# Attention and gated feed-forward block: transposed inputs, the keys' low part by DMA, and the products for the row maxima on 64 rows each

## The chip, the cores and the metric

One core of one Trainium2 chip runs the whole program. The metric is the device time of one execution in microseconds (us); less is better. The profile is of one execution. PE is TensorE, PEld its weight loads, DVE VectorE, ACT ScalarE, POOL GpSimd, SP the engine that issues most DMAs.

## The reference, cut to what matters

Eight batches, 100 query rows of 128, 1444 context rows of 64, 16 heads of 64.

```python
xh = layernorm(x)                                   # x: (8, 100, 128)
q, k, v = xh @ Wq, ctx @ Wk, ctx @ Wv               # ctx: (8, 1444, 64); 16 heads of 64
attn = softmax(q k^T / 8)                           # 100 x 1444 per head and batch
x = x + tanh(g_xattn) * ((attn v) @ Wo + bo)
y = layernorm(x)
h = silu(fp4(y) @ fp4(w_gate)^T) * (fp4(y) @ fp4(w_up)^T)
out = x + tanh(g_ffn) * fp4(h) @ fp4(w_down)^T      # fp4: blocks of 16, scale, round to a grid
```

## The kernel before, in words

**Folding.** The weights Wq and Wk are folded per head into one 128x64 matrix (`a_all`, key "A"), so the keys of every head are the context itself, and Wv with Wo into `vo`. The scores of a head are then (x_hat A_h) times the context.

**Precision.** Scores are exact to about float32 with reduced operands (float32r): the keys are split into a high part and a low part, so are the queries. `k_hl` holds on partitions 0 to 63 the high part and on 64 to 127 the low part of the transposed context (the rounding copies at L589, the low part at L911 on DVE); `k_h1` holds the high part and, below it, rows of ones (L588). `q_hh` holds the queries' high part twice, `q_ls` their low part and the shift.

**Groups and slots.** Work goes in 16 groups, half a batch's heads each (8 heads x 100 queries = 800 columns). A group has 24 slots: 12 chunks of 120 or 121 keys times two halves of 400 columns. A slot is two score products on PE (L793, 128 partitions, and L794, 71 partitions), then Exp on ACT into `probs` (L648). Two PSUM banks hold scores, so PE is at most two slots ahead of ACT. The product with the context (`attn_pair`, L807) writes one chunk to output partitions 0 to 63 and the other to 64 to 127; each of its float32 products is two records in the trace. Sums over keys are adds on DVE (L935) and POOL (L513).

**Maxima.** Exp needs a shift per query. While group g runs, PE makes for group g+1 the products for the maxima: 7 tiles of 116 queries times 3 parts of 482 keys = 21 products (L746, all 128 partitions: high and low part of the keys against the doubled queries). DVE reduces each (L915), then once more (L946), and a transpose (L749) and L917 put the shift into `q_ls`.

**Order of work.** Every engine has its own written program, walked slot by slot. What is not a score or an `attn_pair` is a use of one of four PSUM banks, a ring (`ring_keys`, `START`, `FINISH`, `ring_use` on each engine): the same list on each engine, and a bank is written again when the use four before it has been read (`ring_free`). The dictionaries `MAX_SLOTS`, `FFN_SLOTS`, `POST_SLOTS`, `CTX_SLOTS` and so on say by hand at which slot what is issued; on PE a slot is scores, ring uses, `attn_pair`. In the 24 slots of an even group the context of the next batch is transposed, in three uses of four transposes (L732).

**Start and end.** `START` transposes Wk, Wq, Wv on PE (L693, L685), makes A (L698) and `vo` (L704, operands on 64 partitions, of 0 to 63 and 64 to 127 in turn), the first keys, and the 21 maxima of group 0. `FINISH` is the feed-forward part of the last batch, a chain of small steps over DVE, POOL, ACT and PE.

Of the kernel before, what the change touches and what calls it, by code (L numbers as in the profile page):

```python
# [45 lines left out]
MAXC = [0, 482, 964, M]  # L46
PROBS = 6
# [3 lines left out]
SUM_P = [1, 2, 4, 5, 6, 7, 8]  # L51
# [14 lines left out]
MAX_SLOTS = {1: 1, 2: 1, 4: 1, 5: 2, 7: 3, 8: 2, 10: 2, 11: 2, 12: 1, 13: 2, 14: 1, 15: 1, 16: 1, 17: 1}  # L66
FFN_SLOTS = {2: ('zT', 0), 4: ('gate', 0), 6: ('up', 0)}
DOWN_SLOTS = {2: ('hT', 0), 3: ('hT', 1), 5: ('down', 0)}
LAST_FFN_SLOTS = {**FFN_SLOTS, 19: ('hT', 0), 20: ('hT', 1), 22: ('down', 0)}
W_SLOTS = {slot: ("wT", i) for i, slot in enumerate(LAST_FFN_SLOTS)}  # L70
POST_SLOTS = {6: ('sum', 0), 8: ('proj', 0), 10: ('proj', 1)}
CTX_SLOTS = {14: ('ctx', 0), 15: ('ctx', 1), 18: ('ctx', 2)}
XT_SLOT = 20
MAX_TILES_SLOT = 17
SHIFT_SLOT = 20


LN2_SLOTS = [12, 13]
LN2_APPLY_SLOT = 17
Z_SLOTS = [19, 19, 20, 21, 21, 21, 22, 22, 22]  # L80
SIGMOID_SLOTS = [5, 6]
H_SLOTS = [18, 19, 19, 20, 21, 21, 22, 22, 23]
LAST_H_SLOTS = [7, 8, 9, 10, 11, 12, 13, 14, 16]
ADD_LAG, LAST_ADD_SLOT = 3, 0


def ring_keys(g, slot):
    keys = []
    pre = g + 1 < GROUPS
    if pre and slot == 0:  # L90
# [19 lines left out]
START = [("wkT", 0), ("wqT", 0), ("xT", 0), ("A", 0), ("ctx", 0), ("q", 0), ("ctx", 1)]  # L110
BETWEEN = {1: ('ctx', 2), 4: ('wqT', 1), 7: ('A', 1), 9: ('wvT', 0), 13: ('vo', 0), 14: ('vo', 1), 16: ('vo', 2), 20: ('vo', 3)}
for _u in range(3 * TILES):
    START += ([BETWEEN[_u]] if _u in BETWEEN else []) + [("max", _u)]
START += [("shift", 0)]
FINISH = [("proj", 0), ("proj", 1), ("sum", 0), ("zT", 0), ("gate", 0), ("up", 0), ("hT", 0), ("hT", 1), ("down", 0)]
# [55 lines left out]
def xattn_ffn(nc, x, ctx_in, g_xattn, g_ffn, Wq, Wk, Wv, Wo, bo, w_gate, w_up, w_down, out):  # L171
    with ExitStack() as es:
# [18 lines left out]
        shift_mask = sb("shift_mask", [128, TILES, TROWS])  # L191
        tanh_x = sb("tanh_x", [128, 1])
# [21 lines left out]
        ctx_n = sb("ctx_n", [128, 2, CHUNKS, 2, C])  # L214
# [38 lines left out]
        wk_in = sem("wk_in")  # L253
        wq_in = sem("wq_in")
# [4 lines left out]
        ctx_loaded = [sem(f"ctx_loaded{i}") for i in range(2)]  # L259

# [9 lines left out]
        ctx_copied = sem("ctx_copied")  # L270
# [116 lines left out]
        def _(sp):  # L387
            def load_ctx(b, par):
                for i in range(2):
                    sp.dma_start(ctx_n[0:PFULL, par, :, i, :], ctx_in[b, 0:PFULL * CHUNKS, :].rearrange("(p c) d -> p c d", c=CHUNKS)).then_inc(ctx_loaded[par], 16)  # L390
                    sp.dma_start(ctx_n[PFULL:PFULL + 1, par, 0:EXTRA, i, :], ctx_in[b, PFULL * CHUNKS:M, :].rearrange("(p c) d -> p c d", c=EXTRA)).then_inc(ctx_loaded[par], 16)
# [27 lines left out]
            def group(t):  # L419
                if t.g % 2 == 0 and t.g + 2 < GROUPS:  # L420
# [20 lines left out]
        def _(pool):  # L441
# [72 lines left out]

            def group(t):
                for c in range(CHUNKS):
                    if c == 2 and t.g % 2 == 0 and t.g + 2 < GROUPS:
                        rstd_of(stats[:, 0, :], 0, ln1_stats, 2 * t.batch(2), ln1_eps, ln1_rstd, t.batch(2))
                        residual(t.batch(1), t.parity(1), t.fills(1))
                    if c == 7 and t.g % 2 == 0 and t.g >= 2:  # L520
                        ln2_rows(t)
                    if t.g % 2 and t.g >= 3 and c in (1, 2, 4):
                        swiglu(pool, t, (1, 2, 4).index(c))
                    if t.g == 0 and c in (4, 9):
                        weights_fp4(pool, 3 if c == 4 else 7)
                    if c == 5 and t.g >= 1:
# [5 lines left out]
            def finish(t):  # L532
                ln2_rows(t)
# [5 lines left out]
        def _(act):  # L539
            def ring_use(t, key):  # L540

                kind, k = key
                if kind not in ("wqT", "wkT", "wvT", "A", "vo", "wT", "q", "ctx", "xT", "zT", "proj", "gate", "up", "hT"):
                    return
                if key == ("wqT", 0) or kind == "proj" and t.g == GROUPS:
# [4 lines left out]
                if kind == "wqT" and k == 1:  # L550
                    act.activation(wqT[:, 4 * k:4 * k + 4, :], src, ACT.Copy).then_inc(free, 1)
                elif kind == "wkT":
                    for r in range(2):
                        rows = slice(r * C, (r + 1) * C)
                        op = act.activation(wkT[rows, :, r, :], src[rows, :].rearrange("p (j c) -> p j c", c=C), ACT.Copy)
                    op.then_inc(free, 1)
                elif kind == "wvT":
                    act.activation(wvT[:, :, 0, :], src, ACT.Copy)
                    act.activation(wvT[:, :, 1, :], src, ACT.Copy).then_inc(free, 1)
                elif kind == "A":  # L560
# [17 lines left out]
                elif kind == "q":  # L578
                    half = (t.g + 1) % 2
                    for r in range(2):  # L580
                        cols, heads = slice(r * HALF, (r + 1) * HALF), src[64 * r:64 * r + C, 0:HALF]
                        act.activation(q_hh[64 * r:64 * r + C, half, cols], heads, ACT.Copy).then_inc(q_hi_done, 1)
                        act.activation(q_hh[64 - 64 * r:64 - 64 * r + C, half, cols], heads, ACT.Copy).then_inc(q_hi_done, 1)  # L583
                elif kind == "ctx":
                    a, b = COFF[4 * k], COFF[4 * k + 4]
                    par = t.parity(1)
                    if t.g >= 0:
                        act.activation(k_h1[par][0:C, a:b], src[0:C, 0:b - a], ACT.Copy)  # L588
                    act.activation(k_hl[par][:, a:b], src[:, 0:b - a], ACT.Copy).then_inc(k_hi_done, 1)  # L589
# [5 lines left out]
                elif kind == "proj":  # L595
                    if k == 0:
                        wait_reads(act, (t, ("sum", 0)))
                        if t.g >= 2:
                            act.wait_ge(head_done, t.count(4, -4))
                    for i in range(4):  # L600
                        h = 4 * k + i
                        op = act.activation(head_out[0:N, h, :], src[0:N, i * D:(i + 1) * D], ACT.Copy, scale=rsum[0:N, h:h + 1])  # L602
                    op.then_inc(free, 1)
# [10 lines left out]

            act.wait_ge(consts_v, 1)
            act.activation(unused[0:1, 1:2], unused[0:1, 1:2], ACT.Exp)
            act.wait_ge(consts_v, 2)
            for key in START:
                ring_use(Turn(-1), key)
                if key == ("ctx", 2):  # L620
# [3 lines left out]
                    act.wait_ge(k_hi_done, 3)  # L624
                    act.activation(k_h1[0][0:C, :], k_hl[0][0:C, :].bitcast(F32), ACT.Copy).then_inc(ctx_copied, 1)
# [431 lines left out]
```

## Time and profile before

| what | value |
|---|---|
| median of 3 runs | 572.76 us (571.93 to 573.5) |
| the profiled execution | 572.5 us |
| its span, first to last instruction | 570.7 us |
| mean granted TensorE clock | 0.97 |
| start-up, to the first score product | 36.3 us |
| group 6 (even), group 7 (odd) | 32.64 us, 31.23 us |
| after the last score product | about 29.5 us |

The span is cut at 36.3 us (first score) and 541.2 us (behind the last); the 16 groups lie between. A group's start is read off its first q product (L725) at slot 0. In a timeline, a row of PE starts when its product enters the array, or at its weight load where that could not be made ahead; the stated length includes the pipeline behind it, so that lengths overlap, and costs are read as the difference of two starts.

### The profile page before, as it was taken

Reading aid. Unit: us, or ns where it says so; the run is one execution under the profiler, and the core shown is the slowest. Engines: PE = TensorE matmul, PEld = TensorE weight load, DVE = VectorE, ACT = ScalarE, POOL = GpSimd, SP = SyncE. Lnnn points to the kernel's source line nnn. Section 1 sums busy time; section 2 is a strip of 40 time slices with the busy share of each in tenths; the row PEclk is TensorE's granted clock in tenths of the full one; section 3 lists DMA queues with packets and bytes.
Section 4 is the critical chain, followed back from the end, with each engine's and each line's share of the span. In section 5 each row is a group of like instructions: output and inputs, shape, how many; then the busy total and the mean of one; then the engine's idle time right before and its main releaser. Section 6 shows DMA issues by size and latency. Waiting matters only on the chain.

```text
span 570.7 us, 8404 instructions
## 1 busy us (share of the span) xinstructions
PE 534.2 (94%) x2841; PEld 333.0 (58%) x2841; DVE 433.4 (76%) x769; ACT 311.2 (55%) x731; POOL 272.2 (48%) x251
## 2 busy tenths in 40 slices
PE   5779999999999999999999999999999999999832
PEld 4555565666656565656566565656566565656421
DVE  2768876779786887779796887779787887776745
ACT  3444564666565754566565755566565755546411
POOL 4007427292735456292735456282735365284700
PEclk9789999999999999999999999999999999999975
DMA  8600000300011000300021000300020000000000
GB/s 154 114 1 0 2 1 0 57 2 1 1 38 23 1 1 1 61 0 1 0 48 15 0 1 1 61 1 0 2 56 1 1 2 0 5 1 2 4 1 4
DMA packets 27898, 9.45 MB, mean 17 GB/s; under 512 B 24016, under 2 KB 27600, under 8 KB 27856
## 3 DMA queue, kind: packets, MB, share of 16 engines
q1 hardware_dynamic: 27856, 8.92, 8.5%
q8 instruction: 23, 0.38, 0.3%
q14 instruction: 19, 0.16, 0.1%
HBM read 8.50 MB, written 0.41 MB: 16 GB/s over the span
## 4 chain that ended last, share of the span: by engine, by line
PE 82%; DVE 10%; issue 3%; ACT 3%; POOL 1%; DMA 1%; SPq 0%; POOLq 0%; ACTq 0%; DVEq 0%
PE attn L807 24%; PE scores L793 16%; PE ring L746 12%; PE scores L794 11%; PE ring L760 5%; PE ring L753 4%; DVE max L915 3%; PE ring L725 3%; PE ring L732 2%; DVE acc_v L935 2%; PE ring L766 2%; ACT q_hh L583 1%; PE ring L774 1%; PE ring L749 1%; DMA x_in<-in_x 1%
## 5 line engine op out<-in xcount | busy, mean ns | idle before, releaser
L648 ACT ACTIVATE probs<-scores 120x400 f32<-120x400 f32 (+1 forms) x384 | 186.5, 504 | 193.0 <-PE scores L794 190.2
L915 DVE TENSOR_REDUCE max<-ring 116x1 f32<-116x482 f32 (+1 forms) x336 | 205.1, 653 | 57.7 <-PE ring L746 54.2
L513 POOL TENSOR_TENSOR acc_p<-acc_p,probs 120x800 f32<-120x800 f32 x79 | 152.7, 1934 | 71.7 <-ACT probs L648 65.8
L807 PE MATMUL attn<-probs,ctx_n 120*64 120x400 f32 (+1 forms) x768 | 171.8, 526 | 0.0
L793 PE MATMUL scores<-q_hh,k_hl 128*120 128x400 f32 (+1 forms) x384 | 153.5, 400 | 1.2 <-DVE q_ls L917 1.2
L793 PEld LDWEIGHTS scores<-q_hh,k_hl 128*120 128x120 f32 (+1 forms) x384 | 70.2, 183 | 125.6 <-ACT probs L648 72.0
L794 PE MATMUL scores<-q_ls,k_h 71*120 71x400 f32 (+1 forms) x384 | 133.9, 349 | 0.0
L746 PE MATMUL ring<-k_hl,q_hh 128*116 128x482 f32 (+1 forms) x336 | 119.5, 411 | 5.7 <-DVE k_hl L911 2.3
L794 PEld LDWEIGHTS scores<-q_ls,k_h 71*120 71x120 f32 (+1 forms) x384 | 70.9, 185 | 4.2
L746 PEld LDWEIGHTS ring<-k_hl,q_hh 128*116 128x116 f32 (+1 forms) x336 | 58.2, 182 | 16.6 <-DVE max L915 7.0
L807 PEld LDWEIGHTS attn<-probs,ctx_n 120*64 120x64 f32 (+1 forms) x768 | 38.1, 135 | 46.4 <-issue 34.4
L935 DVE TENSOR_TENSOR acc_v<-acc_v,probs 120x800 f32<-120x800 f32 x49 | 48.9, 999 | 1.4 <-ACT probs L648 0.7
L454 POOL TENSOR_TENSOR stats<-stats,eps 100x1 f32<-100x1 f32 x16 | 3.0, 189 | 97.9 <-DVE stats L886 97.9
L513 POOL TENSOR_TENSOR acc_p<-probs 121x800 f32<-121x800 f32 x16 | 30.2, 1888 | 22.3 <-ACT probs L648 22.3
L602 ACT ACTIVATE head_out<-ring,rsum 100x128 f32<-100x128 f32 x120 | 34.3, 368 | 10.8 <-PE ring L760 10.8
L474 POOL TENSOR_TENSOR head_out<-head_out 100x512 f32<-100x512 f32 (+2 forms) x45 | 37.2, 827 | 2.9
L376 POOL TENSOR_TENSOR e_gate<-e_gate,ones 100x352 f32<-100x352 f32 x7 | 5.4, 776 | 62.9 <-ACT gate L606 62.9
L760 PE MATMUL ring<-vo,attn_sb 128*100 128x128 f32 x256 | 33.1, 272 | 0.0
L760 PEld LDWEIGHTS ring<-vo,attn_sb 128*100 128x100 f32 x256 | 31.5, 166 | 1.2 <-issue 0.7
L905 DVE TENSOR_TENSOR q_ls<-ring,q_hh 64x400 fp32r<-64x400 f32 x32 | 18.3, 571 | 14.1 <-ACT q_hh L583 13.7
L911 DVE TENSOR_TENSOR k_hl<-ring,k_hl 64x480 fp32r<-64x480 f32 (+1 forms) x24 | 15.9, 662 | 14.6 <-ACT k_hl L589 14.4
L753 PEld LDWEIGHTS ring<-ones,acc_v 121*100 121x100 f32 x256 | 25.0, 168 | 2.0
(129 smaller groups left out, 484.2 us busy)
## 6 DMA issues: line engine op xcount, KB each, us to landing
ctx_n<-in_ctx SPq DMA_DIRECT2D x16, 360.0 KB
wq<-in_L_xattn_Wq SPq DMA_DIRECT2D x1, 512.0 KB, 4.6
wo<-in_L_xattn_Wo SPq DMA_DIRECT2D x1, 512.0 KB, 7.2
x_in<-in_x SPq DMA_DIRECT2D x8, 50.0 KB
out<-y_out SPq DMA_DIRECT2D x8, 50.0 KB
wk<-in_L_xattn_Wk SPq DMA_DIRECT2D x1, 256.0 KB, 3.8
ctx_n<-in_ctx SPq DMA_DIRECT2D x16, 1.0 KB
wv<-in_L_xattn_Wv SPq DMA_DIRECT2D x1, 256.0 KB, 6.2
```

The lines of the kernel that those rows point to most:

```text
L474: pool.tensor_tensor(head_out[0:N, 0:n, :], head_out[0:N, 0:n, :], head_out[0:N, n:2 * n, :], ALU.add).then_inc(head_done, 1)
L513: pool.tensor_tensor(acc_p[0:r, t.g % 2, :], left, probs[0:r, c % PROBS, :], ALU.add).then_inc(sum_p, 1)
L602: op = act.activation(head_out[0:N, h, :], src[0:N, i * D:(i + 1) * D], ACT.Copy, scale=rsum[0:N, h:h + 1])
L648: act.activation(probs[0:r, c % PROBS, k * HALF:(k + 1) * HALF], scores[0:r, slot % SCORE_BANKS, 0:HALF], ACT.Exp).then_inc(probs_full, 1)
L746: mm = pe.matmul(dst[0:rows, 0:b - a], q_hh[:, (t.g + 1) % 2, tile * TROWS:tile * TROWS + rows], k_hl[par][:, a:b], start=True, stop=True)
L753: mm = pe.matmul(dst[0:N, h:h + 1], acc_v[0:CROWS[0], (t.g + 1) % 2, h * N:(h + 1) * N], ones[0:CROWS[0], 0:1], start=True, stop=True)
L760: mm = pe.matmul(dst[0:N, i * D:(i + 1) * D], attn_sb[:, h * N:(h + 1) * N], vo[:, HG * ((t.g + 1) % 2) + 2 * i + k, :], start=True, stop= ...
L793: pe.matmul(dst, k_hl[par][:, a:a + r], q_hh[:, half, cols], start=True, stop=False)
L794: pe.matmul(dst, k_h1[par][0:C + TILES, a:a + r], q_ls[0:C + TILES, half, cols], start=False, stop=True).then_inc(scores_full, 1)
L807: mm = pe.matmul(attn[64 * i:64 * i + C, k, 0:HALF], ctx_n[0:r, par, c, 0, :], probs[0:r, c % PROBS, k * HALF:(k + 1) * HALF], start=(j == ...
L915: dve.tensor_reduce(max3[0:rows, tile, part:part + 1], src[0:rows, 0:MAXC[part + 1] - MAXC[part]], AX.X, ALU.max).then_inc(free, 1)
L935: dve.tensor_tensor(acc_v[0:r, t.g % 2, :], left, probs[0:r, c % PROBS, :], ALU.add).then_inc(sum_v, 1)
```

## The change

The host hands in the context also transposed (`ctxT`) and the weights Wq, Wk, Wv transposed. The loads are reordered, x first, and two of them are issued by ACT. So the weight transposes, the context transposes (key "ctx") and their copies go. The keys are now made from `ctxT` in SBUF by six copies on ACT per batch (`copy_k`): minus the rounded high part into `k_hl[0:64]`, the high part into `k_h1[0:64]` and `k_hl[64:128]`. A DMA from POOL's queue that adds (`split_k`) turns the first into the low part. `ctx_n` is loaded once instead of twice. The products for the maxima use the high part of the keys alone: products with an even number read partitions 0 to 63 (`k_h1`), those with an odd number 64 to 127 (`k_hl`). `vo` is made in group 0 instead of in the start-up. The lists of slots are new, `attn_pair` has a list of its own, ACT's q copies, key copies and head scalings are placed slot by slot, and products into a free bank (`keep_warm`) are put at the start and at two places of the end. In the last part the layer norm is applied on DVE instead of by POOL and ACT, and one product of the feed-forward on POOL.

```diff
+KC = [0, M // 2, M]
...
-MAX_SLOTS = {1: 1, 2: 1, 4: 1, 5: 2, 7: 3, 8: 2, 10: 2, 11: 2, 12: 1, 13: 2, 14: 1, 15: 1, 16: 1, 17: 1}
-FFN_SLOTS = {2: ('zT', 0), 4: ('gate', 0), 6: ('up', 0)}
+MAX_SLOTS = [{1: 2, 4: 1, 5: 1, 6: 1, 7: 4, 8: 1, 11: 2, 12: 2, 13: 2, 14: 1, 16: 2, 17: 2}, {1: 1, 3: 2, 6: 1, 7: 4, 8: 1, 9: 1, 10: 2, 13: 1, 14: 2, 15: 4, 17: 1, 18: 1}]
+FFN_SLOTS = {1: ('zT', 0), 3: ('gate', 0), 4: ('up', 0)}
...
-CTX_SLOTS = {14: ('ctx', 0), 15: ('ctx', 1), 18: ('ctx', 2)}
+VO_SLOTS = {3: ('vo', 0), 5: ('vo', 1), 9: ('vo', 2), 13: ('vo', 3)}
...
+PV_SLOTS = [4, 6, 8, 11, 12, 14, 16, 18, 21, 22, 24, 26]
+HEAD_SLOTS = [7, 7, 8, 9, 9, 9, 9, 9]
+CTX_COPY_SLOTS = [7, 7, 11, 11, 12, 12]
+KLO_AT = 8
+WARM = [2, 6, 6]
...
-START = [("wkT", 0), ("wqT", 0), ("xT", 0), ("A", 0), ("ctx", 0), ("q", 0), ("ctx", 1)]
-BETWEEN = {1: ('ctx', 2), 4: ('wqT', 1), 7: ('A', 1), 9: ('wvT', 0), 13: ('vo', 0), 14: ('vo', 1), 16: ('vo', 2), 20: ('vo', 3)}
+START = [("xT", 0), ("A", 0), ("q", 0), ("A", 1)]
...
-FINISH = [("proj", 0), ("proj", 1), ("sum", 0), ("zT", 0), ("gate", 0), ("up", 0), ("hT", 0), ("hT", 1), ("down", 0)]
+FINISH = [("proj", 0), ("sum", 0), ("proj", 1), ("zT", 0), ("gate", 0), ("up", 0), ("hT", 0), ("hT", 1), ("down", 0)]
...
+            def split_k(t):
+                b = t.batch(1)
+                pool.wait_ge(k_hi_done, 6 * b - 2)
...
+                pool.dma_start(k_hl[b % 2][0:C, :], ctxT_in[b, :, :], accum_op=ALU.add).then_inc(k_lo_done, 16)
...
+            def copy_k(t, step):
+                part, par = step % 2, t.parity(1)
+                cols = slice(KC[part], KC[part + 1])
...
+                key = (k_hl[par][0:C, cols], k_h1[par][0:C, cols], k_hl[par][C:128, cols])[step // 2 if t.g >= 0 else 1]
+                act.activation(key, ctxT[:, cols], ACT.Copy, scale=-1.0 if t.g >= 0 and step < 2 else 1.0).then_inc(k_hi_done, 1)
...
-                for c in range(4 * k, 4 * k + 4):
-                    r, a = CROWS[c], COFF[c] - COFF[4 * k]
-                    mm = pe.transpose(dst[:, a:a + r], ctx_n[0:r, par, c, :, :].rearrange("p i d -> p (i d)"), ident[0:r, 0:r])
...
-                    mm = pe.matmul(dst[0:rows, 0:b - a], q_hh[:, (t.g + 1) % 2, tile * TROWS:tile * TROWS + rows], k_hl[par][:, a:b], start=True, stop=True)
+                    keys, at = (k_hl[par], slice(C, 128)) if k % 2 else (k_h1[par], slice(0, C))
+                    mm = pe.matmul(dst[0:rows, 0:b - a], q_hh[at, (t.g + 1) % 2, tile * TROWS:tile * TROWS + rows], keys[at, a:b], start=True, stop=True)
...
+            def keep_warm(times):
+                for _ in range(times):
+                    pe.matmul(scores[:, 0, :], ident[:, :], ones[:, 0:1].to_broadcast([128, 512]), start=True, stop=True)
...
                 if slot == 0:
+                    if t.g % 2 == 0:
+                        pe.wait_ge(k_hi_done, 6 * t.batch(1) - 4)
...
+                            pe.wait_ge(k_lo_done, 16 * t.batch())
...
-                    dve.tensor_tensor(k_hl[par][C:128, a:b], src[C:128, 0:b - a], k_hl[par][C:128, a:b].bitcast(F32), ALU.subtract).then_inc(free, 1)
...
+                if key == ("max", 2):
+                    dve.tensor_tensor(k_hl[0][0:C, :], ctxT[:, :], k_h1[0][0:C, :].bitcast(F32), ALU.subtract).then_inc(first_lo, 1)
+                    for r in range(2):
+                        split_q(Turn(-1), r)
...
+    views["ctxT"] = inputs["ctx_512"][:, keys, :].transpose(0, 2, 1)
+    for name in ("Wq", "Wk", "Wv"):
+        w = inputs["L0_xattn_" + name]
+        views[name + "T"] = w.T.reshape(HG, 128, w.shape[0]).transpose(1, 0, 2)
```

## Rows read from the trace of the kernel before

**Rows 1.** The page: busy time, clock, chain by engine, largest DVE group

```profile
PE 534.2 (94%) x2841; PEld 333.0 (58%) x2841; DVE 433.4 (76%) x769; ACT 311.2 (55%) x731; POOL 272.2 (48%) x251
...
PEclk9789999999999999999999999999999999999975
...
PE 82%; DVE 10%; issue 3%; ACT 3%; POOL 1%; DMA 1%; SPq 0%; POOLq 0%; ACTq 0%; DVEq 0%
...
L915 DVE TENSOR_REDUCE max<-ring 116x1 f32<-116x482 f32 (+1 forms) x336 | 205.1, 653 | 57.7 <-PE ring L746 54.2
```

**Rows 2.** Busy time of each engine by stretch, PEclk the granted clock

```profile
36.30:68.60 32.30, 30.27 (x133) 17.47 (x134) 27.27 (x41) 16.26 (x34) 18.15 (x11) 0.89 0.00 1
226.31:258.95 32.64, 32.43 (x182) 20.65 (x182) 25.64 (x50) 19.94 (x49) 16.42 (x17) 1.00 0.15 27
258.95:290.18 31.23, 31.23 (x166) 19.01 (x165) 25.50 (x45) 17.84 (x43) 16.79 (x13) 1.00 0.01 2
```

**Rows 3.** Timeline of PE, steady state: start us, length us, operation

```profile
206.39 0.82 PE L746 MATMUL ring<-k_hl,q_hh 128*116 128x480 f32 x3
207.04 0.34 PE L793 MATMUL scores<-q_hh,k_hl 128*120 128x400 f32 x1
...
208.81 0.56 PE L807 MATMUL attn<-probs,ctx_n 121*64 121x400 f32 x2
...
216.36 0.38 PE L746 MATMUL ring<-k_hl,q_hh 128*116 128x480 f32 x1
216.67 0.89 PE L807 MATMUL attn<-probs,ctx_n 120*64 120x400 f32 x4
217.49 0.44 PE L793 MATMUL scores<-q_hh,k_hl 128*120 128x400 f32 x1
217.77 0.34 PE L794 MATMUL scores<-q_ls,k_h 71*120 71x400 f32 x1
```

**Rows 4.** Timeline of PEld (weight loads), same stretch

```profile
216.66 0.20 PEld L807 LDWEIGHTS attn<-probs,ctx_n 120*64 120x64 f32 x4 [0.30 <-issue]
```

**Rows 5.** Timeline of PE in the start-up, around products that read 64 partitions

```profile
26.14 0.47 PE L746 MATMUL ring<-k_hl,q_hh 128*116 128x482 f32 x1 [0.29 <-ACT wvT L559]
26.54 1.16 PE L704 MATMUL ring<-wo,wvT 64*128 64x128 f32 x8
27.63 0.47 PE L746 MATMUL ring<-k_hl,q_hh 128*116 128x482 f32 x1
```

**Rows 6.** Timeline of PEld, same stretch

```profile
26.54 0.96 PEld L704 LDWEIGHTS ring<-wo,wvT 64*128 64x128 f32 x8 [0.23 <-issue]
27.62 0.18 PEld L746 LDWEIGHTS ring<-k_hl,q_hh 128*116 128x116 f32 x1
```

**Rows 7.** Timeline of PE around the context transposes of an even group

```profile
249.72 0.57 PE L732 MATMUL ring<-ident,ctx_n 120*128 120x120 f32 x4
250.06 0.45 PE L746 MATMUL ring<-k_hl,q_hh 128*104 128x482 f32 x1
```

**Rows 8.** Timeline of all engines, start-up

```profile
6.45 0.29 DVE L882 BATCH_NORM_STATS2 stats<-x_in 100x6 f32<-100x128 f32 x1 [3.98 <-DMA x_in<-in_x]
...
17.26 0.66 DVE L915 TENSOR_REDUCE max<-ring 116x1 f32<-116x482 f32 x1
...
34.41 0.17 DVE L946 TENSOR_REDUCE maxes<-max 116x7 f32<-116x21 f32 x1
...
36.30 0.41 PE L793 MATMUL scores<-q_hh,k_hl 128*121 128x400 f32 x1 [1.21 <-DVE q_ls L917]
```

**Rows 9.** Timeline of all engines, last group and end

```profile
536.61 0.36 PE L770 MATMUL ring<-ident,h_fp 100*128 100x100 f32 x2 [1.82 <-DVE h_fp L364]
...
550.91 0.49 ACT L635 ACTIVATE z<-y,offset,rstd 100x128 f32<-100x128 f32 x1 [7.64 <-POOL offset L464]
...
554.98 1.47 PE L766 MATMUL ring<-gateT,zT 128*100 128x352 f32 x2 [0.43 <-ACT zT L594]
...
566.71 1.57 PE L774 MATMUL ring<-downT,hT 128*100 128x128 f32 x6 [0.49 <-ACT hT L613]
```

More of the change, by code:

```diff
@@ L46 @@
 MAXC = [0, 482, 964, M]
+KC = [0, M // 2, M]
+KQ = [M // 4 * i for i in range(5)]
 PROBS = 6
@@ L50 @@
 SUM_V = [0, 3, 9, 10, 11]
-SUM_P = [1, 2, 4, 5, 6, 7, 8]
+SUM_P = [c for c in range(CHUNKS) if c not in SUM_V]
 ADDS_V, ADDS_P = len(SUM_V), len(SUM_P) - 1
@@ L89, in ring_keys @@
     pre = g + 1 < GROUPS
-    if pre and slot == 0:
+    if pre and slot == Q_SLOT:
         keys += [("q", 0)]
@@ L250, in xattn_ffn @@
         y_out = sb("y_out", [128, 2, D])
-        wk_in = sem("wk_in")
-        wq_in = sem("wq_in")
+        qk_in = [sem(f"qk_in{i}") for i in range(2)]
         wvo_in = sem("wvo_in")
@@ L549, in ring_use @@
                 act.wait_ge(ring_full[bank], n)
[L550 to L560, printed above, removed]
+                if kind == "A":
                     heads = src.rearrange("p (h c) -> p h c", c=C)
@@ L594, in ring_use @@
                     act.activation(zT[:, :], src[:, 0:N], ACT.Copy).then_inc(free, 1)
[L595 to L603, printed above, removed]
                 elif kind == "gate":
@@ L756, in ring_use @@
                     if k == 0 and t.g == 1:
-                        wait_reads(pe, *[(Turn(-1), ("vo", part)) for part in range(4)], own=bank)
+                        wait_reads(pe, *[(t.before(), ("vo", part)) for part in range(4)], own=bank)
                     for i in range(4):
@@ L889, in ln_apply, with split_first_k, split_q @@
                 dve.tensor_scalar(dst, src, stat[0:N, 6:7], rstd[0:N, which:which + 1], ALU.subtract, ALU.mult).then_inc(done, 1)
+            def split_first_k(part):
+                cols = slice(KC[part], KC[part + 1])
+                dve.wait_ge(k_hi_done, part + 1)
+                dve.tensor_copy(k_hl[0][C:128, cols], k_h1[0][0:C, cols]).then_inc(k_first, 1)
+            def split_q(t, r):
+                half, (bank, n) = (t.g + 1) % 2, t.ring(("q", 0))
+                rows, cols = slice(64 * r, 64 * r + C), slice(r * HALF, (r + 1) * HALF)
+                if r == 0:
+                    dve.wait_ge(ring_full[bank], n)
+                dve.wait_ge(q_hi_done, t.count(4, 4 + 2 * r + 2))
+                op = dve.tensor_tensor(q_ls[0:C, half, cols], ring[rows, bank, 0:HALF], q_hh[rows, half, cols].bitcast(F32), ALU.subtract)
+                if r == 1:
+                    op.then_inc(ring_free[bank], 1)
             def ring_use(t, key):
                 kind, k = key
-                if kind not in ("q", "ctx", "max", "shift", "sum", "down") and key != ("wqT", 0):
+                if kind not in ("max", "shift", "sum", "down") and key != ("A", 0):
                     return
@@ L983, in group @@
                 for slot in range(SLOTS):
+                    for r in [i for i in range(2) if Q_LO_SLOTS[i] == slot and t.g + 1 < GROUPS]:
+                        split_q(t, r)
                     for key in ring_keys(t.g, slot):
                         ring_use(t, key)
-                    if slot == MAX_TILES_SLOT and t.g + 1 < GROUPS:
+                    if slot == MAX_TILES_SLOT[t.g % 2] and t.g + 1 < GROUPS:
                         max_tiles(t)
```

284 lines of the change are left out of this document (160 added, 124 removed).

## The prediction

> **What bounds the kernel now.** I read the page first [rows 1]: PE is busy 94% of the span and is 82% of the chain of waits, the clock is granted in full except in the first slices and at the end, and the next engine, DVE, is at 76%. Then the stretches [rows 2]: in groups 6 and 7 PE is busy 32.43 of 32.64 us and all 31.23 of 31.23 us, DVE 25.6 and 25.5, ACT 19.9 and 17.8. So in the steady state only PE's own stream counts: what it saves or adds is the time saved or added, and DVE, ACT and POOL have 5 us and more of room in each group. Group 0 is the exception, with 2.0 us of idle PE [rows 2].
>
> "Busy" hides what matters here, so I read starts, not lengths [rows 3]. Three products for the maxima and nothing else take 206.39 to 207.04: 0.22 us each. A score product whose weights are loaded ahead takes about 0.18. Around the context products the stream is dearer. The product for the maxima at 216.36 is followed by them only at 216.67, 0.31 instead of 0.22, and their weight load is not made ahead: it starts at 216.66, after 0.30 us in which PEld had nothing that the trace shows [rows 4]. Behind them the score product starts at 217.49 and the next at 217.77: 0.28 instead of 0.18. I read this as a change of how the array is divided: PE first runs empty, 0.09 us, and then the next weights are loaded in the open, 0.10 us for 120 columns and about 0.05 for 64.
>
> **Does the same hold for products on 64 partitions?** The start-up has the nearest rows: the `vo` products (L704) read 64 partitions and stand between full-height products [rows 5]. The one at 26.14 is followed at 26.54, 0.40 us later, and the weight load stands at the same 26.54, behind 0.23 us in which PEld had nothing that the trace shows [rows 6]. Of the 0.40, 0.22 is the product and 0.10 its own late load, so 0.08 is emptying. Eight records of L704 then take 1.09 to the next start, and that product's load (27.62) again stands at its own start. All four `vo` uses show it, with the lower and the upper 64 alike. So yes: in and out both cost. **Price of one switch between full height and 64 rows: 0.09 + 0.10 = 0.19 us.** Lower bound 0.14 (0.09 with the short load of 64 columns).
>
> The Trainium skill says the same in one sentence that speaks against this change, "Mode switching requires drain" (TensorEngine Tiling (Array Packing), Key Properties). It gives no duration, so the sum does not use it. [Rows 3, 5] agree with it, by 0.08 to 0.09 us.
>
> **Products for the maxima, the main term.** I count runs in the new MAX_SLOTS. An even group has 12 runs of 2, 1, 1, 1, 4, 1, 2, 2, 2, 1, 2, 2; seven of them (slots 4, 6, 8, 11, 12, 14, 16) stand directly before an `attn_pair`, where a switch is paid anyway, so they add one switch, and five add two: 17. An odd group has runs of 1, 2, 1, 4, 1, 1, 2, 1, 2, 4, 1, 1; four (slots 6, 8, 14, 18) stand before an `attn_pair`: 4 + 16 = 20 switches. 17 x 0.19 = 3.23 us and 20 x 0.19 = 3.80 us.
> Against that, two neighbours in a run use different halves of the array and different banks and can flow together. No row shows this for halves by rows. Bounds: nothing gained, or two in the time of one. I take the second, by the nearest row, the context products, which use halves by columns: in the stretch cut at 208.9 the first two records, one for each half, span 0.56 us together and all four of 216.67 span 0.89, 0.33 more: two steps of 0.33, not four, with the halves of a step side by side [rows 3]. The even group then has 13 steps for 21 products (saves 8 x 0.22 = 1.76), the odd one 14 (saves 7 x 0.22 = 1.54). Net +1.47 and +2.26 us. Groups 0 to 14 make maxima, 8 even and 7 odd: 11.8 + 15.8 = **+27.6 us**.
>
> **Context transposes.** Three uses of four transposes, each 249.72 to 250.06 = 0.34 us [rows 7], in seven even groups: 21 x 0.34 = **-7.1 us**. What replaces them is off PE: ACT has six copies of 722 columns instead of six of 480, 1 to 2 us more per batch against 12 us of room; DVE loses three subtractions a batch. The low part by DMA is issued at POOL's chunk 8 of the even group and is first read by the scores of the next batch, more than one group (31 us) later; with that much time it costs nothing, and if it were late PE would wait at slot 0 of seven groups. POOL's wait for ACT's copies (slot 11) stands behind its chunk 7, with the adds of chunk 8 queued behind it; the copies are done by then.
>
> **`vo` moved into group 0.** Four uses of 1.09 - 0.19 = 0.90 us, and four switches (slots 3 and 9; slots 5 and 13 share those of the maxima): 3.6 + 0.8 = **+4.4 us**, less 1.0 us of the 2.0 idle in group 0 (between 0 and 2; half, as part of it is the wait for the shift at the first slot): **-1.0**.
>
> **Start-up.** The first reduction is at 17.26, the last is followed by L946 at 34.41, scores begin at 36.30 [rows 8]. The 17.15 us in between hold 21 x 0.653 = 13.7 of reductions [rows 1] and 3.4 of waits and splits. After: x is asked for first and not third (its landing at 6.45 comes 1.2 us earlier), the weight transposes and their copies are gone (about 2 us more), so the first reduction comes near 14.0; 13.7 of reductions stay, and the low parts of keys (about 2 us) and queries (1.1 us) now stand among them. 14.0 + 13.7 + 3.1 + 1.9 = 32.7, rounded with what the warm-up products may do for the clock to **-4 us** (0 to -7).
>
> **Last group and end.** The 1.8 us wait for h_fp at 536.61 shrinks, since gate, up and sigmoid are earlier: **-1.5** (0 to -2). In the end chain two POOL steps and ACT's z fall out for one DVE step (about 0.6), one DVE product goes to POOL (0.5), and if the clock stays full the gate product (554.98, 0.6 us) and the down products (566.71, 0.8 us) are halved [rows 9]; other small ones 0.5: **-3** (-1 to -4). The warm-up products stand on PE beside small steps of the other engines, for which PE waits anyway (from ACT's z at 550.91 to the gate product at 554.98, for one); at half clock they could still run when zT is wanted, and cost 1 to 2 us, the -1 end.
>
> **Sum.** 27.6 - 7.1 + 4.4 - 1.0 - 4 - 1.5 - 3 = +15.4 us. Made against the profiled execution, 572.5 us: 587.9; the median of the runs is 0.3 higher, so 588.2. I say **588.0**. Ends of this case: with 0.14 a switch, 276 switches (17 x 8 + 20 x 7) cost 13.8 less: 574. If the second weight load of a run stands behind the first instead of beside it, 98 runs of two or more add 9.8, and with nothing won in the start-up 4 more: 602.
>
> **Rivals.**
> 1. **The halves don't flow together.** Switches are paid and the 1.76 and 1.54 us are not saved: + 8 x 1.76 + 7 x 1.54 = +24.9, 613. For it: no row shows two row halves at once. Against: the column halves do.
> 2. **Faster: the switch costs nothing for these products.** They are float32r with 482 columns, while L704 is float32 and follows other work. If the chip treats them as full-height products, they cost what they cost, and the rest remains: 7.1 + 4 + 1.5 + 3 + 1.0 - 3.6 = 13 us less, 560. The point from which it decides: 276 p - 24.9 - 12.2 = 0, p = 0.134 us a switch with halves together. Against it: both neighbours of every `vo` use.
> 3. **Free switches and halves together.** 560 - 24.9 = 535. DVE's 25.5 us would still fit in groups of 29.
> The skill's table (TensorEngine Tiling (Array Packing), Theoretical Speedup) allows "Up to 2x" for a small dimension of 64 and lists no cost beside it; alone, that is this third case. [Rows 5, 6] speak against it.
> A wait that takes a place: a run of four needs all four banks, and DVE frees one in 0.65 us while PE fills two in 0.22. There are 8 + 14 = 22 such runs; at up to 0.65 each +14. It is inside the range of the main case.
>
> **How the numbers follow.** Main case 0.70 (574 to 602), first rival 0.12, second 0.10, third 0.08. The range reaches to the second rival and leaves out the first and third, 0.20: 560 to 602. A measurement of this kernel can tell 0.3%, 1.7 us. Faster: 0.18 and the tip of the main case, 0.20. Slower: most of the main case and the first rival, 0.76. Same: 0.04.
>
> **What the profile after would show.** Right: groups near 33 us with PE busy throughout; between a score product and one for the maxima 0.27 to 0.3 us instead of 0.18, with the weight load at the product's own start; the two products of a pair starting within 0.02 us; first score near 32 us. Wrong: weight loads of L746's successor made ahead, or groups below 31 us (rivals 2, 3); pairs 0.2 us apart (rival 1); long waits of PE for DVE's maxima.

## The result, and the profile after

The changed kernel takes 621.5 us (median of 4 runs, 619.6 to 631.5) against 573.1 before: ratio 1.084, interval 1.079 to 1.088. Slower, as forecast, but by 48 us instead of 15, and outside the range of 560 to 602. The run at 631.5 us had a lower granted clock than the other three (0.89 against 0.91), and the ratio is of those three, whose median is 620.2. The profiled execution took 620.2 us, span 618.4, against 572.5 and 570.7.

The page of the kernel after, for [rows 1]:

```profile
PE 597.4 (97%) x2749; PEld 316.9 (51%) x2749; DVE 434.2 (70%) x749; ACT 315.3 (51%) x722; POOL 285.3 (46%) x264
...
PEclk9555579989899998979999999989998999989998
...
PE 90%; DVE 6%; issue 2%; ACT 1%; POOL 0%; DVEq 0%; ACTq 0%; POOLq 0%
...
L964 DVE TENSOR_REDUCE max<-ring 116x1 f32<-116x482 f32 (+1 forms) x336 | 206.0, 652 | 113.7 <-PE ring L770 113.2
```

PE is still the bound, now busy 97%, and DVE has become less so. What [rows 1] had not shown is in the second row: the clock is at half, a full run of fives, from the second slice to the fifth, and below full again and again behind it. The mean is 0.91 against 0.97.

I cut both kernels at the same places, by the first q product of a group: start-up and first slot, group 0, groups 1 to 13, groups 14 and 15, the end. The columns are start:end, us, then busy us (instructions) of PE, PEld, DVE, ACT, POOL, then the granted clock, DMA share and GB/s. After:

```profile
0.00:29.50 29.50, 19.17 (x55) 10.53 (x56) 20.57 (x38) 6.13 (x12) 8.84 (x20) 0.73 0.63 138
29.50:84.90 55.40, 54.90 (x153) 27.53 (x152) 24.75 (x39) 21.16 (x39) 18.22 (x13) 0.50 0.07 14
84.90:530.00 445.10, 442.72 (x2159) 235.10 (x2159) 330.40 (x567) 252.00 (x583) 224.49 (x202) 0.97 0.08 16
530.00:590.90 60.90, 60.32 (x309) 33.36 (x307) 42.77 (x67) 32.52 (x81) 32.13 (x26) 0.97 0.01 2
590.90:618.40 27.50, 20.23 (x80) 10.37 (x78) 15.70 (x40) 3.52 (x9) 1.66 (x3) 0.93 0.02 4
```

and before:

```profile
0.00:36.70 36.70, 24.62 (x118) 18.80 (x119) 19.80 (x37) 13.62 (x24) 6.96 (x20) 0.91 0.59 104
36.70:68.90 32.20, 30.17 (x135) 17.37 (x134) 27.57 (x42) 16.48 (x35) 18.15 (x11) 0.89 0.00 1
68.90:481.70 412.80, 411.77 (x2230) 256.23 (x2229) 325.58 (x587) 244.15 (x583) 213.54 (x190) 1.00 0.07 13
481.70:540.90 59.20, 57.17 (x309) 34.08 (x308) 44.95 (x67) 32.97 (x81) 32.48 (x26) 1.00 0.01 2
540.90:570.70 29.80, 10.45 (x56) 6.50 (x54) 15.55 (x40) 4.02 (x10) 1.12 (x4) 0.65 0.02 4
```

| stretch | before | after | difference |
|---|---|---|---|
| start-up | 36.7 | 29.5 | -7.2 |
| group 0 | 32.2 | 55.4 | +23.2 |
| groups 1 to 13 | 412.8 | 445.1 | +32.3 |
| groups 14 and 15 | 59.2 | 60.9 | +1.7 |
| end | 29.8 | 27.5 | -2.3 |

Group 0 is at half clock from end to end (0.50), groups 1 to 13 have a mean clock of 0.97. What that costs is read from groups with and without half clock in them. Here are an even and an odd group of the kernel after without, and an even one with:

```profile
187.20:220.30 33.10, 32.72 (x170) 17.74 (x170) 25.76 (x47) 21.30 (x49) 17.44 (x19) 1.00 0.16 35
291.30:325.00 33.70, 33.70 (x167) 17.18 (x166) 26.30 (x45) 17.82 (x43) 17.51 (x13) 1.00 0.01 2
255.30:291.30 36.00, 35.60 (x171) 19.96 (x170) 25.89 (x47) 21.34 (x49) 17.44 (x19) 0.91 0.15 34
```

Seven odd and six even groups without half clock are 7 x 33.7 + 6 x 33.1 = 434.5 us, so of the 445.1 about 11 are clock. A mean of 0.97 means 2 x 0.03 x 445 = 27 us at half clock: one microsecond at half clock costs about 0.4 us, not 0.5. Not all work takes twice as long there: two score products behind a load in the open start 0.28 us apart at full clock (239.75 and 240.03 below) and 0.49 at half (40.13 and 40.62), and such a load lasts 0.18 and 0.28 us. By this price group 0 loses 0.4 x 55.4 = 22 us where before 3 were lost (2 x 0.11 x 32.2 = 7 us at half clock), and groups 14 and 15 lose 1. So some 31 of the 48 us are clock. This is an estimate from the granted clock and the groups of this run.

Now the step in question, at full clock, for [rows 3 to 6]. Timeline of PE and of PEld of the kernel after, in an odd group:

```profile
239.07 0.34 PE L830 MATMUL scores<-q_ls,k_h 71*120 71x400 f32 x1
239.34 0.47 PE L770 MATMUL ring<-k_h,q_hh 64*116 64x482 f32 x1
239.35 0.47 PE L770 MATMUL ring<-k_hl,q_hh 64*116 64x480 f32 x1
239.75 0.44 PE L829 MATMUL scores<-q_hh,k_hl 128*120 128x400 f32 x1
240.03 0.34 PE L830 MATMUL scores<-q_ls,k_h 71*120 71x400 f32 x1
```

```profile
239.34 0.17 PEld L770 LDWEIGHTS ring<-k_h,q_hh 64*116 64x116 f32 x1 [0.27 <-issue]
239.34 0.17 PEld L770 LDWEIGHTS ring<-k_hl,q_hh 64*116 64x116 f32 x1
239.74 0.18 PEld L829 LDWEIGHTS scores<-q_hh,k_hl 128*120 128x120 f32 x1 [0.23 <-issue]
```

The two products of the run start within 0.01 us of each other and so do their loads: the halves flow together. The score product before them starts at 239.07 and they at 239.34, 0.27 us, and behind them 239.75 to 240.03 is 0.28: both loads are made in the open, on either side. That is the switch as forecast.

### The profile page after: what moved, and what is told of

The parts are those of the page before. It is cut to its first block, busy times and chain, and to the rows that moved or that the text cites. A ratio compares the mean times of both kernels' runs of the same rounds, so it can differ in the third digit from the quotient of the medians.

```text
span 618.4 us, 8174 instructions
## 1 busy us (share of the span) xinstructions
PE 597.4 (97%) x2749; PEld 316.9 (51%) x2749; DVE 434.2 (70%) x749; ACT 315.3 (51%) x722; POOL 285.3 (46%) x264
## 4 chain that ended last, share of the span: by engine, by line
PE 90%; DVE 6%; issue 2%; ACT 1%; POOL 0%; DVEq 0%; ACTq 0%; POOLq 0%
PE attn L844 26%; PE scores L829 21%; PE ring L770 14%; PE scores L830 11%; PE ring L784 6%; PE ring L777 3%; DVE max L964 3%; PE ring L754 2%; PE ring L790 2%; PE ring L733 1%; PE ring L798 1%; PE ring L773 1%; PE scores L804 1%; PE ring L727 0%; DVE e_gate L922 0%
## 5 line engine op out<-in xcount | busy, mean ns | idle before, releaser
L844 PE MATMUL attn<-probs,ctx_n 120*64 120x400 f32 (+1 forms) x768 | 179.9, 549 | 0.0
L829 PE MATMUL scores<-q_hh,k_hl 128*120 128x400 f32 (+1 forms) x384 | 170.9, 445 | 1.3 <-DVE q_ls L966 1.2
L770 PE MATMUL ring<-k_h,q_hh 64*116 64x482 f32 (+3 forms) x176 | 84.7, 501 | 5.0 <-DVE q_ls L948 3.9
L770 PE MATMUL ring<-k_hl,q_hh 64*116 64x482 f32 (+2 forms) x160 | 77.2, 506 | 0.0
L770 PEld LDWEIGHTS ring<-k_h,q_hh 64*116 64x116 f32 (+1 forms) x176 | 31.3, 186 | 34.3 <-issue 24.8
L495 POOL TENSOR_TENSOR head_out<-head_out 100x512 f32<-100x512 f32 (+2 forms) x45 | 43.4, 964 | 2.4
L784 PE MATMUL ring<-vo,attn_sb 128*100 128x128 f32 x256 | 40.6, 311 | 0.0
L770 PEld LDWEIGHTS ring<-k_hl,q_hh 64*116 64x116 f32 (+1 forms) x160 | 28.6, 191 | 21.8 <-issue 18.3
L784 PEld LDWEIGHTS ring<-vo,attn_sb 128*100 128x100 f32 x256 | 37.5, 197 | 2.7 <-DVE max L964 1.6
L580 ACT ACTIVATE q_hh<-ring 64x400 fp32r<-64x400 f32 x64 | 31.9, 499 | 8.1 <-PE ring L754 7.0
L948 DVE TENSOR_TENSOR q_ls<-ring,q_hh 64x400 fp32r<-64x400 f32 x32 | 18.3, 571 | 16.6 <-ACT q_hh L580 15.4
```

The costliest lines, as they stand in the source:

```text
L495: pool.tensor_tensor(head_out[0:N, 0:n, :], head_out[0:N, 0:n, :], head_out[0:N, n:2 * n, :], ALU.add).then_inc(head_done, 1)
L580: act.activation(q_hh[rows, half, cols], ring[64 * r:64 * r + C, bank, 0:HALF], ACT.Copy).then_inc(q_hi_done, 1)
L770: mm = pe.matmul(dst[0:rows, 0:b - a], q_hh[at, (t.g + 1) % 2, tile * TROWS:tile * TROWS + rows], keys[at, a:b], start=True, stop=True)
L784: mm = pe.matmul(dst[0:N, i * D:(i + 1) * D], attn_sb[:, h * N:(h + 1) * N], vo[:, HG * ((t.g + 1) % 2) + 2 * i + k, :], start=True, stop= ...
L829: pe.matmul(dst, k_hl[par][:, a:a + r], q_hh[:, half, cols], start=True, stop=False)
L844: mm = pe.matmul(attn[64 * i:64 * i + C, k, 0:HALF], ctx_n[0:r, par, c, :], probs[0:r, c % PROBS, k * HALF:(k + 1) * HALF], start=(j == 0) ...
```

## The experiments

E1 was run four times and E10 seven times; E2 to E9 are one execution each. The four executions of the changed kernel lie 12 us apart, so small differences between single runs are read only where the stretches of the trace show them.

Theory A at this point: the loss is the 64-row products, by their switches and by a clock that falls because they are in the stream. Rival B: the half clock comes from the new start and from `vo` in group 0.

**E1, full height.** The whole change, but products for the maxima on 128 partitions:

```diff
-keys, at = (k_hl[par], slice(C, 128)) if k % 2 else (k_h1[par], slice(0, C))
+keys, at = k_hl[par], slice(0, 128)
...
+pe.wait_ge(first_lo, 1)                     # start-up
+pe.wait_ge(k_lo_done, 16 * t.batch(1))      # odd groups
...
-if key == ("max", 2):                       # DVE: first low part of the keys
+if key == ("max", 0):
```

> The changed kernel with its products for the maxima back at full height (high and low keys on 128 partitions against the doubled queries); all else stays, the new slots, start and end too. Theory A (the loss is the 64-row products: the switches, and a clock that falls because they are in the stream): about 557 us, granted clock back to 0.95 or more, group 0 near 33 us, no half-clock stretches inside the groups, weight loads ahead of the maxima's products. Theory B (the half clock from 14 to 85 us comes from the new start and from vo in group 0, not from the products' height): the switches' 28 us go but group 0 stays near 50 us at half clock, about 575 to 585 us.

566.3 us, ratio to the kernel before 0.989 (0.984 to 0.993). The same stretches of it, without the end:

```profile
0.00:28.70 28.70, 18.46 (x55) 9.92 (x56) 20.86 (x38) 6.13 (x12) 7.56 (x20) 0.77 0.63 142
28.70:68.90 40.20, 38.45 (x154) 22.98 (x153) 26.95 (x37) 20.41 (x39) 19.89 (x13) 0.78 0.10 20
68.90:479.10 410.20, 406.00 (x2159) 246.98 (x2158) 331.15 (x570) 250.27 (x583) 225.13 (x202) 1.00 0.08 18
479.10:537.30 58.20, 57.33 (x309) 33.73 (x307) 43.04 (x67) 32.56 (x81) 32.16 (x26) 1.00 0.01 2
```

So the 64-row products cost 55 us, and the rest of the change gains 6, about 1%. Groups 1 to 13 are at full clock throughout; an even one takes 31.9 us (162.5 to 194.5), an odd one 31.4 (257.8 to 289.2). Theory A holds; but group 0 has half clock here too (2 x 0.22 x 40.2 = 18 us of it, about 7 us lost), so B has a small share.

**E2, lower half only**, to price the pairs: `keys, at = k_h1[par], slice(0, C)` for every product.

> The changed kernel with all products for the maxima on partitions 0 to 63, none on 64 to 127: as many switches, but no two side by side. If halves side by side are worth what their starts say, each of the 15 second products per batch (21 x 2 - 27) costs 0.22 us at full clock: 8 x 1.76 + 7 x 1.54 = 25 us more than the changed kernel, about 645 us, two products of a run 0.2 us apart. If the clock falls for the emptier array, it falls as often or more. If pairs were worth nothing: 620 us.

```profile
28.70:86.10 57.40, 56.90 (x153) 28.88 (x153) 24.83 (x39) 21.14 (x39) 18.21 (x13) 0.50 0.07 13
86.10:599.70 513.60, 512.34 (x2159) 270.75 (x2159) 342.03 (x567) 253.94 (x583) 225.34 (x202) 0.86 0.07 14
```

691.3 us, 70 more than the changed kernel and 46 more than I expected. An odd group at full clock takes 35.5 us against 33.7, 1.8 more where 1.54 was worked out, and an even one (529.6 to 564.2, clock 0.99) 34.6 against 33.1, 1.5 more where 1.76 was. Over groups 1 to 13 that is 7 x 1.8 + 6 x 1.5 = 21.6 us, as worked out. These groups take 513.6 - 445.1 = 68.5 us more, so the other 47 are clock: granted 0.86 instead of 0.97, with as many switches as in the changed kernel. Pairs save time twice, by their own length and by keeping the clock.

**E3, fewer runs.** The same 64-row products, 8 runs a group, each ahead of an `attn_pair`:

```diff
+MAX_SLOTS = [{4: 2, 6: 2, 8: 1, 11: 4, 12: 2, 14: 4, 16: 4, 18: 2}, {4: 2, 6: 2, 8: 2, 11: 4, 12: 2, 14: 4, 16: 4, 18: 1}]
```

> The changed kernel with the same 64-row products in fewer runs: 8 per group, each directly before an attn_pair (even slots 4:2, 6:2, 8:1, 11:4, 12:2, 14:4, 16:4, 18:2; odd 4:2, 6:2, 8:2, 11:4, 12:2, 14:4, 16:4, 18:1), so 16 switches a batch instead of 37 and 22 steps instead of 27. Switch price 0.19 and step 0.22: 4.0 + 1.1 = 5.1 us less per batch, 38 us in all at full clock: about 583 us, or less if the half-clock stretches shrink too. Rival (DVE is asked for four maxima at a time and PE waits for banks): at least half of that is given back, 600 us or more, with waits of PE for DVE max of over 10 us.

```profile
29.60:80.10 50.50, 47.61 (x153) 25.15 (x152) 25.59 (x39) 20.71 (x39) 19.30 (x13) 0.60 0.08 15
80.10:509.30 429.20, 423.40 (x2158) 234.28 (x2158) 328.85 (x567) 245.17 (x583) 219.31 (x202) 0.97 0.08 17
```

```profile
PEld ring L770 <- DVE max L964: 17.1, 50, 1.0
```

603.5 us, 18 less and not 38. The odd groups drop from 33.7 to 31.3 us, as short as E1's; 2.4 less where 12 x 0.19 + 3 x 0.22 = 2.9 was worked out. The even groups, 33.1 us at full clock in the changed kernel, now take 33.6: PE is idle 1.5 us in one of them (244.3 to 277.9) instead of 0.4, and loads for the maxima wait 17.1 us in all for DVE to free a bank. What takes the rest of the 2 us that fewer switches should save there stays open. The expected rival has come: 603.5, waits of over 10 us. Groups 1 to 13 still have a mean clock of 0.97, with less than half of the added switches.

**E4, the kernel before with 64 rows.** One edit: its products read partitions 0 to 63 only, high parts alone. No transposed inputs, no new start.

```diff
-... q_hh[:, ...], k_hl[par][:, a:b], ...
+... q_hh[0:C, ...], (k_hl if t.g < 0 else k_h1)[par][0:C, a:b], ...
```

> The kernel before with one edit: its products for the maxima read partitions 0 to 63 only (high parts, no pairs), slots as before. Its 14 runs per group, 7 of them before an attn_pair (4, 8, 10, 12, 14, 16, and 2): 7 + 7 x 2 = 21 switches, 0.19 each = 4.0 us per group, 15 groups: 60 us more, 632 us at full clock. If the height of the products pulls the clock down by itself, half-clock stretches appear inside the groups here too and it is above 640; if only the new start did that, none do.

```profile
40.50:92.40 51.90, 51.40 (x134) 23.92 (x134) 26.67 (x42) 16.90 (x35) 17.06 (x11) 0.53 0.00 1
92.40:641.90 549.50, 549.50 (x2230) 292.38 (x2229) 327.75 (x586) 247.36 (x583) 212.91 (x190) 0.81 0.05 10
```

754.0 us, 182 more than the kernel before by this one edit. Odd groups at full clock are 34.9 to 35.0 us (31.2 before, +3.7; 4.0 worked out), and the clock falls to a mean of 0.81 over groups 1 to 13. Of the 549.5 - 412.8 = 137 us that these take more, 13 x 3.7 = 48 are the switches and the other 89 clock. Nothing else of the change is needed to lose the clock.

Is it the height, or the emptying at the switches? **E5** keeps full height and adds the switches: ahead of each run one product of 64 partitions and 8 columns into the same bank.

```diff
 (on E1)
+if k in FIRST_OF_RUN[t.g % 2]:
+    pe.matmul(dst[0:rows, 0:8], q_hh[0:C, (t.g + 1) % 2, tile * TROWS:tile * TROWS + rows], k_h1[par][0:C, a:a + 8], start=True, stop=True)
```

> E1 (full height) with one product of 64 partitions and only 8 columns, into the same bank, ahead of each run of maxima; the full-height product then overwrites it. So every run has two switches (24 a group, more than the changed kernel's 17 and 20) while the array's work stays that of E1. Price 0.19 a switch and some 0.03 for the small product: 12 x 0.41 = 4.9 us a group, 15 groups, 74 us over E1: about 640 us. Theory C (the clock falls with the emptying at the switches): half-clock stretches inside the groups as in the changed kernel or more, 660 us or more. Theory D (it falls with the products' height, that is with how much of the array works): none beyond those of E1, groups near 36.5 us.

```profile
31.40:91.90 60.50, 60.00 (x166) 32.98 (x166) 24.55 (x39) 21.16 (x39) 18.21 (x13) 0.50 0.07 13
91.90:570.70 478.80, 476.32 (x2315) 279.83 (x2314) 337.01 (x567) 253.12 (x583) 224.53 (x202) 0.97 0.07 15
```

661.7 us, in the range of theory C. Group 0 is at half clock from end to end, groups 1 to 13 at 0.97, as in the changed kernel, although all large products are at full height. So theory D as I put it falls: low products of full length are not needed, switches between full-height products bring the half clock too. It also prices them: groups without half clock take 36.0 (even, 352.6 to 388.6) and 35.7 us (odd, 535.0 to 570.7), 4.1 and 4.3 over E1's 31.9 and 31.4; less 12 small products of an estimated 0.03, and over 24 switches, that is 0.16 us a switch.

**E6 and E7, when.** Full height in the start-up and group 0 only (`if t.g <= 0`), and from group 1 on only (`if t.g > 0`).

> The changed kernel with full-height products in the start-up and in group 0 only, 64 rows in groups 1 to 14. If the long half-clock stretch at the start (14 to 85 us) needs the 64-row products there: group 0 as in E1 (40 us, 18 of them at half clock), the short dips of later groups stay, so about 15 us less than the changed kernel: 603 to 607. If it comes from something else in the start, no change: 620.

> The reverse: 64 rows in the start-up and in group 0, full height from group 1 on. Group 0 as in the changed kernel (55 us, all at half clock), all later groups as in E1 (31.4 and 31.9): 566 + 15 = 581 us. If the later groups' dips were set off by something other than the height of their own products, dips stay and it is above 590.

```profile
28.70:67.90 39.20, 38.70 (x154) 23.38 (x154) 24.24 (x37) 20.41 (x39) 19.04 (x13) 0.76 0.10 20
67.90:513.50 445.60, 443.16 (x2158) 235.30 (x2157) 333.55 (x570) 252.02 (x583) 224.74 (x202) 0.97 0.08 16
```

```profile
28.80:84.30 55.50, 55.00 (x154) 27.62 (x153) 24.74 (x39) 21.20 (x39) 18.21 (x13) 0.50 0.07 14
84.30:494.90 410.60, 406.43 (x2159) 247.41 (x2157) 328.71 (x567) 249.82 (x583) 224.91 (x202) 1.00 0.08 18
```

604.1 and 582.5 us, both as expected. E7's group 0 takes 15.3 us more than E1's, of which 1.5 are switches: the clock is the rest. The two parts are independent: 64 rows in the start-up and group 0 cost 16 us there (E7 over E1), in groups 1 to 14 they cost 38 (E6 over E1). The sum, 54, is the 55 of the whole, so I see no sign that one stretch carries its state into the other.

**E8, entering group 0 warm.** Six full-height products of 512 columns where PE waits in the start-up.

```diff
 for key in START:
+    if key[0] == "shift":
+        keep_warm(6)
```

> The changed kernel with six warm-up products (512 columns, float32, full height) ahead of the start-up's shift, where PE waits for DVE. If group 0 is at half clock only because it is entered so (a state that the mix with 64-row products can keep but not leave): group 0 near 38 us and the total 17 us less, less up to 5 us for the products at half clock, about 608. If the mix of group 0 itself pulls the clock down, it falls again within a few us: 620 or more.

```profile
24.50 8.10 PE L804 MATMUL scores<-ones,ident 128*128 128x512 f32 x12
...
34.10 0.41 PE L831 MATMUL scores<-q_hh,k_hl 128*121 128x400 f32 x1 [1.21 <-issue]
34.35 0.35 PE L832 MATMUL scores<-q_ls,k_h 71*121 71x400 f32 x1
...
37.44 0.69 PE L831 MATMUL scores<-q_hh,k_hl 128*121 128x400 f32 x1
37.93 0.54 PE L832 MATMUL scores<-q_ls,k_h 71*121 71x400 f32 x1
```

626.7 us. The first scores of group 0 (34.10 to 34.35, 0.25) are at full clock, three microseconds later (37.44 to 37.93, 0.49) they are at half, and group 0 ends 54.7 us long. The mix of group 0 pulls the clock down; entering it at full clock gains under 1 us. The start-up is 5.0 us longer by the added products.

**E9, more work per run.** The changed kernel with a full-height float32 product of 256 columns ahead of each run; its result is overwritten.

```diff
+if t.g >= 0 and k in FIRST_OF_RUN[t.g % 2]:
+    pe.matmul(dst[:, 0:256], ident[:, :], ones[:, 0:1].to_broadcast([128, 256]), start=True, stop=True)
```

> The changed kernel with one full-height float32 product of 256 columns (0.21 us at full clock) into the same bank ahead of each run of maxima in groups 0 to 14; switches, pairs and 64-row products stay. It adds 12 x 0.21 = 2.6 us a group, 39 us in all at full clock: 660 us with the half-clock stretches as they are. If the clock follows how much work reaches the array on average: fewer or no dips in groups 1 to 14 (27 us of half clock there now), group 0 leaves the half clock, and it ends near or under 640. If it follows the switches by number: dips as before, 655 us or more.

```profile
29.20:77.60 48.40, 47.90 (x178) 26.96 (x178) 23.92 (x38) 20.47 (x39) 18.30 (x13) 0.74 0.08 16
77.60:581.00 503.40, 503.40 (x2470) 279.06 (x2469) 328.55 (x569) 254.83 (x583) 223.94 (x202) 0.99 0.07 14
```

674.6 us. I had the product's length wrong: each float32 product is two records (E8's six are x12), and it takes 0.43 and not 0.21 us, 77 us in all. Against 620 + 77 = 697 it is 22 less, and that is clock: group 0 at 0.74 instead of 0.50, groups 1 to 13 at 0.99 instead of 0.97, with every switch in place. So the number of switches does not decide by itself either; full-height work around them brings much of the clock back. It also spreads them (20 switches in an odd group of 39 us instead of 34), so that their number per microsecond falls too.

**E10, fillers at full height.** E1 with fillers where PE waits for DVE in the start-up: one product of 160 columns ahead of each maximum from the third on, two of 512 ahead of the shift, one behind it.

```diff
 (on E1)
 for key in START:
+    if key[0] == "max" and key[1] >= 2:
+        pe.matmul(scores[:, 0, 0:160], ident[:, :], ones[:, 0:1].to_broadcast([128, 160]), start=True, stop=True)
+    elif key[0] == "shift":
+        keep_warm(2)
     ring_use(Turn(-1), key)
+keep_warm(1)
```

> E1 with filler products where PE waits for DVE in the start-up: one of 160 columns ahead of each of the maxima's products from the third on, two of 512 ahead of the shift and one behind it. E1 has half clock from 12 to 19 and from 23 to 47 us. If the fillers keep the clock up into group 0: group 0 takes 31 to 34 us instead of 40 and the total is 559 to 562 us, 2% under the kernel before. If group 0's own mix (vo on 64 partitions, waits for ACT) pulls it down: no gain, 565 to 568.

```profile
0.00:29.00 29.00, 22.65 (x98) 16.80 (x99) 20.98 (x38) 6.13 (x12) 7.56 (x20) 0.94 0.63 141
29.00:67.10 38.10, 35.57 (x155) 20.52 (x154) 26.93 (x37) 20.26 (x39) 19.90 (x13) 0.87 0.11 21
67.10:477.40 410.30, 406.07 (x2158) 246.95 (x2158) 331.25 (x570) 250.29 (x583) 225.13 (x202) 1.00 0.08 18
```

561.8 us, ratio 0.981 (0.979 to 0.984) to the kernel before: faster than both, though whether by 2% is open. Group 0 is entered at full clock and falls to half for 10 us (34.1 to 44.3). It takes 38.1 us and not the 31 to 34 expected, 2.1 less than in E1, with a clock of 0.87 instead of 0.78. The profiled execution (565.2) was the slowest of its seven: its mean clock is 0.982, that of the others 0.989 to 0.992, and at 0.4 us for each of the some 10 us less at half clock that is about the 4 us between them. Where they keep the clock no trace shows.

## Why the prediction was right or wrong

**Right: the bound, the switch and the pair.** "Only PE's own stream counts" held. Price 0.19 us: the rows of after show 0.27 and 0.28 where 0.18 is undisturbed, and 0.41 where the product alone would take 0.22, which is 0.38 for two switches; E5 gives 0.16 on average. The pairs start together, the first rival (613) is out, and so are the second and third: loads are not made ahead. The net of the main term for groups 1 to 13 was 7 x 2.26 + 6 x 1.47 = 24.6 us; measured at full clock against E1, 434.5 - 410.2 = 24.3. The Trainium skill's "Mode switching requires drain" (TensorEngine Tiling (Array Packing), Key Properties) is borne out, by 0.09 us of emptying at each switch; its "Up to 2×" for a dimension of 64 (Theoretical Speedup) holds for a pair by itself, whose second product costs 0.01 us here, and not for the kernel.

**Wrong: the clock.** The step that failed stands in the first paragraph of the argument, "the clock is granted in full except in the first slices and at the end". That was read off the kernel before and then used for the kernel after as if it were a property of the chip: half clock inside the groups is a term that was put at nothing without a reason, and the range had no case in which it appears. The runs show in its place about 31 us (19 in group 0, 11 in groups 1 to 13, 1 in the last two). The terms forecast come, by stretch, to -4, +3.9, +18.5, 0 and -3; measured are -7.2, +23.2, +32.3, +1.7 and -2.3. So group 0 is 19.3 us over and groups 1 to 13 are 13.8 over, of which 11 are clock. With the 31 taken off, the change costs 17 us, against 15.4 forecast. That it comes so close is in part luck: 3.2 us more were won in the start-up and 3.5 fewer in groups 1 to 13 by what is not the maxima, and the two nearly cancel.

Where the clock goes: E1 and E4 show that the 64-row products lose it, in this kernel and in the one before. E5 shows that switches between full-height products are enough, E9 that full-height work around the same switches brings much of it back. The number of switches is not the measure: E2 has as many as the changed kernel and a clock of 0.86 instead of 0.97, E3 has 16 added ones a batch instead of 37 and the same 0.97. Work thinned out in the array by low products and by emptying would fit these runs; that is argued and not measured.

The sign did not hang on the clock. It was said to turn at 0.134 us a switch; at E5's 0.16 the sum is still +7 us at full clock.

**The smaller terms.** Start-up: -7.2 against -4 (range to -7); x lands so early that its statistics start at 2.81 us, where I had taken 5.2 from a load that stood behind two others in [rows 8]. `vo` and the context: E1's groups 1 to 13 gain 2.6 us where 6 x 1.02 = 6.1 were expected; PE is idle 4.2 us there against 1.0 before, so most of the difference turned into short waits. Group 0 of E1: 18 us at half clock, about 7 us, not forecast. End: -2.8 (E1) against -3. Low part of the keys by DMA: landed in 4.9 us, no wait of PE for it, nothing, as said. One count was off: the new lists have 8 x 7 + 7 x 5 = 91 runs of two or more and not 98, which puts the upper end at 601 instead of 602 and changes nothing else.

**Expectations that missed.** E1 by 9 us, E2 by 46, E4 by 122, mostly for the same reason, a clock carried over from the kernel before it. E3 missed its main case by 20 and E8 by 19, and E5 ended 22 over its price at full clock; in all three the rival that was named beside it came true. E9 missed by the length of a product, E10 in the length of group 0.

## What to carry to other kernels

A change that thins out a full TensorE stream has two prices: the time it adds, and the clock it may lose. Price it at full clock, then ask what it comes to at half clock for a group or more, and give that case a chance; here it was the larger term. Nor is a share of the clock the same share of the time: here a microsecond at half clock cost 0.4 us and not 0.5. A pair of split products saved 0.22 us and a switch cost 0.16 to 0.19, and a run that stood alone paid it twice. By these prices splitting the array can pay only where the split products stand in long runs or beside work that is split anyway; no run here was faster by it, and at full clock E3's odd groups only drew level with full height (31.3 and 31.4 us).

## What was unexpected of the hardware

- A stream can be busy 99% of the time and still be at half clock: in group 0 of the changed kernel PE is busy 54.9 of 55.4 us, granted clock 0.50 throughout. It takes no stream of 64-row products (E5 has only short ones), and the number of switches alone does not decide it (E9 has all of them, E3 fewer than half). What does is left open.
- One edit to a good kernel, 64 instead of 128 partitions in 336 of 2841 PE records (E4), took it from 572 to 754 us, 89 of them by clock in groups 1 to 13 alone.
- At full clock the penalty of a switch is the same for float32r products of 482 columns as for the float32 `vo` products of 128 in [rows 5], and the same on both halves: a run of one between score products starts 0.28 us behind the product before it, is followed after 0.40, and that product after 0.28, whether it reads partitions 0 to 63 or 64 to 127.
